# Feed-forward's quantisation of the gated activations: two ScalarE operations instead of two VectorE operations

## What is computed

```
def _act_quant(x):
    scale = 127.0 / jnp.clip(jnp.max(jnp.abs(x), axis=-1, keepdims=True), 1e-05)
    return jnp.clip(jnp.round(x * scale), -128.0, 127.0) / scale
def _bitlinear(x, w):
    return jnp.einsum('bsi,oi->bso', _act_quant(x), _weight_quant(w))
gate = jax.nn.silu(_bitlinear(x, w_gate))      # 256 -> 1024
up = _bitlinear(x, w_up)                       # 256 -> 1024
return _bitlinear(gate * up, w_down)           # 1024 -> 256
```

## Time and profile before

| | us |
|---|---|
| median of 3 runs | 7127.48 (7126.87 to 7132.86) |
| the profiled execution, its own time | 7131.26 |
| its span, first to last instruction | 7129.5 |
| TensorE busy | 5831.5 (82%) |
| VectorE busy | 5463.8 (77%) |
| ScalarE busy | 3784.8 (53%) |
| GpSimd busy | 2616.1 (37%) |
| mean granted clock of TensorE | 0.917 of full speed |

### The profile page before, as it was taken

How to read it: one execution, slowest core, us unless ns; L and a number is a source line. 1 busy time by engine, 2 the same in 40 slices (tenths; PEclk the granted TensorE clock), 3 DMA queues, 4 the chain that set the end, 5 groups by cost and what they waited for, 6 DMA issues and landing times. The chain is left out here.

```text
span 7129.5 us, 143478 instructions
## 1 busy us (share of the span) xinstructions
PE 5831.5 (82%) x54804; PEld 3904.2 (55%) x54914; DVE 5463.8 (77%) x12626; ACT 3784.8 (53%) x6869; POOL 2616.1 (37%) x2600
## 2 busy tenths in 40 slices
PE   6899898688888787876999999999118888888887
PEld 4666566454545455544666666666105666666655
DVE  6777777578888888887777777777657888888886
ACT  4666666444555555553565565556105555555554
POOL 0111111122222222232434434544315666656664
PEclk9999999888888888887999999999658999999998
DMA  1111111100000000000000000100100000000000
GB/s 54 37 44 40 42 38 37 43 15 23 23 20 23 20 23 19 24 21 26 29 25 27 30 27 24 32 27 22 35 17 24 18 27 21 22 27 18 27 27 12
DMA packets 140386, 194.36 MB, mean 27 GB/s; under 512 B 25808, under 2 KB 63696, under 8 KB 139344
## 3 DMA queue, kind: packets, MB, share of 16 engines
q1 hardware_dynamic: 139728, 185.26, 8.2%
HBM read 113.03 MB, written 72.18 MB: 26 GB/s over the span
## 5 line engine op out<-in xcount | busy, mean ns | idle before, releaser
L1079 DVE TENSOR_REDUCE Dmp<-pj 128x2 f32<-128x512 f32 x1024 | 647.1, 683 | 145.5 <-PE pj L794 143.4
L1079 DVE TENSOR_REDUCE Amp<-pj 128x2 f32<-128x512 f32 x1024 | 644.7, 683 | 136.0 <-PE pj L794 135.6
L1079 DVE TENSOR_REDUCE Cmp<-pj 128x2 f32<-128x512 f32 x1024 | 643.2, 683 | 90.0 <-PE pj L794 89.5
L932 ACT ACTIVATE Dpr<-st 128x512 f32<-128x512 f32 x1024 | 528.8, 603 | 314.4 <-PE st L729 313.5
L932 ACT ACTIVATE Apr<-st 128x512 f32<-128x512 f32 x1024 | 528.7, 602 | 288.2 <-PE st L729 286.5
L932 ACT ACTIVATE Cpr<-st 128x512 f32<-128x512 f32 x1024 | 529.5, 606 | 250.5 <-PE st L729 249.1
L1014 POOL TENSOR_SCALAR Bve<-Bmv 128x2 f32<-128x2 f32 x128 | 29.6, 231 | 1346.0 <-DVE Bmv L1145 1346.0
L1014 POOL TENSOR_SCALAR Ave<-Amv 128x2 f32<-128x2 f32 x64 | 14.7, 229 | 1141.2 <-DVE Amv L1145 1141.2
L990 POOL TENSOR_TENSOR Dnrm<-Dnrm,power 128x32 f32<-128x32 f32 x64 | 348.6, 5447 | 161.7 <-DVE Dnrm L1057 161.7
L729 PE MATMUL st<-Dq,Dk 32*128 32x256 f32 x4096 | 361.7, 433 | 51.0 <-DVE Dq L1086 40.4
L932 ACT ACTIVATE Bpr<-st 77x512 f32<-77x512 f32 x512 | 262.0, 593 | 191.5 <-PE st L729 190.8
(11 more groups left out here) (310 smaller groups left out, 15817.8 us busy)
## 6 DMA issues: line engine op xcount, KB each, us to landing
Ax0T<-in_xT SPq DMA_DIRECT2D x64, 256.0 KB, 2.6
Ax<-in_x SPq DMA_DIRECT2D x64, 256.0 KB, 2.9
x_A_scratch<-Ax SPq DMA_DIRECT2D x64, 256.0 KB, 2.0
Bx<-x_A_scratch SPq DMA_DIRECT2D x64, 256.0 KB, 2.9
x_B_scratch<-Bx SPq DMA_DIRECT2D x64, 256.0 KB, 2.0
Cx<-x_B_scratch SPq DMA_DIRECT2D x64, 256.0 KB, 2.8
x_C_scratch<-Cx SPq DMA_DIRECT2D x64, 256.0 KB, 2.0
Dx<-x_C_scratch SPq DMA_DIRECT2D x64, 256.0 KB
```

What stands on the lines that cost most here:

```text
L932: ck.tell(act.activation(dst, st[bank][0:n, :], ACT.Exp, scale=HD ** -0.5), "probs_ready", step)
L1079: ins = dve.tensor_reduce(dst, src, AX.X, ALU.max, negate=True)
```

## The change

In hq, VectorE stops after the scale (column 11) and the factor (column 10), which are now issued one behind the other without a link between, and signals scale_ready. ScalarE gets a part in hq: it waits for scale_ready, computes hid * scale + MAGIC in place with one ACTIVATE (Identity, scale and bias from SBUF), waits for it, and computes hid - MAGIC into hq with a second one. The upper bound of 127 is left away. MAGIC and -MAGIC lie in a new tile of two columns, filled in the setup. The place of hq in the list is what it was; on ScalarE all its later steps now stand behind it.

```
-        "hq": ["dve_step"] * 6 + ["hq_ready"],
+        "hq": ["dve_step"] * 3 + ["scale_ready", "hid_rounded", "hq_ready"],
...
+        rounding = sb("rounding", [P, 2])
...
+                pool.memset(rounding[:, 0:1], MAGIC)
+                pool.memset(rounding[:, 1:2], -MAGIC)
...
+                    elif kind == "hq":
+                        t = step[3]
+                        flat = hid[s][:].rearrange("p a b -> p (a b)")
+                        ck.wait("scale_ready", step)
+                        ck.tell(act.activation(flat, flat, ACT.Identity, scale=qsc[s][:, t, 11:12], bias=rounding[:, 0:1]),
+                                "hid_rounded", step)
+                        if t > 0:
+                            ck.wait("hqT_ready", ("hT", att, s, t - 1))
+                        ck.wait("hid_rounded", step)
+                        ck.tell(act.activation(hq[s][:], flat, ACT.Identity, bias=rounding[:, 1:2]), "hq_ready", step)
...
-                        link(ck, dve.tensor_scalar(q[:, 11:12], q[:, 9:10], q[:, 6:7], QMAX, ALU.mult, ALU.mult))
-                        link(ck, dve.tensor_scalar(q[:, 10:11], q[:, 8:9], wq_inv[:, 2:3], 1.0 / QMAX,
-                                                   ALU.mult, ALU.mult))
-                        link(ck, dve.tensor_scalar(flat, flat, q[:, 11:12], MAGIC, ALU.mult, ALU.add))
-                        if t > 0:
-                            ck.wait("hqT_ready", ("hT", att, s, t - 1))
-                        ck.tell(dve.tensor_scalar(hq[s][:], flat, MAGIC, QMAX, ALU.subtract, ALU.min), "hq_ready", step)
-                        ck.wait("hq_ready", step)
+                        dve.tensor_scalar(q[:, 11:12], q[:, 9:10], q[:, 6:7], QMAX, ALU.mult, ALU.mult)
+                        ck.tell(dve.tensor_scalar(q[:, 10:11], q[:, 8:9], wq_inv[:, 2:3], 1.0 / QMAX,
+                                                  ALU.mult, ALU.mult), "scale_ready", step)
+                        ck.wait("scale_ready", step)
```

## The result

The changed kernel takes 7558.2 us (7545.79 to 7566.17, 4 runs) against 7128.71 us of the kernel before: ratio 1.060, 95% interval 1.0582 to 1.0618, 430 us more. The forecast was 7423 us with a range of 7270 to 7560; the time lies at its upper end, where the prediction had put "the clock falls too" (7553). The profiled execution took 7566.17 us, its span is 7564.4.

The account below looks back on a forecast made before the run. Stage B was taken as bound by in-order waits between engines, not busy time, though VectorE leads at 86%. Eight place shifts sum to 18.5 us a turn, times 16 is 296 us: 7423 us against the median, range 7270 to 7560.

Parts of the forecast that it names:

- the clock falls too: Rival: longer TensorE idle stretches lower its stage B clock to 0.74, adding 130 us: 7553 us; chance 0.12.
- a: Stream 0, tile 0: ScalarE's exponentials and key copies, formerly done before the scale, now wait behind hq; shift 3.8 us.
- b: Stream 1, tile 0: hq, then a copy and the Tanh VectorE waits for, come later on ScalarE; shift 2.2 us.
- c: Stream 1, tile 1: hq delays two copies of transposed tiles that TensorE's down product waits for; 0.5 us.
- d: Stream 0, tile 1: hq fits into 4.28 us of ScalarE idle time; no shift, and VectorE's relief worth nothing.
- e: Stream 3, tile 0: hq delays the oT copy, Tanh and query copies that free TensorE's bank; shift 1.6 us.
- f: Stream 3, tile 1: hq delays the take copy and the Tanh behind it; shift 1.3 us.
- g: Stream 2, tile 0: four exponentials, on which products and takes hang, now come after hq and a copy; shift 4.9 us.
- h: Stream 2, tile 1: two oT copies that release TensorE's output products now stand behind hq; shift 4.2 us.
- the sum as read: Main case: the shifts of all eight places in stage B add up, giving 7340 to 7500 us; chance 0.60.
- Only the longer path: Rival: ScalarE's queue has more room, leaving only the longer path to each consumer, about 144 us: 7271 us; chance 0.17.
- Relief wins: Rival: ScalarE has slack at most places, so each hq gives back VectorE's 1.5 us: 6935 us; chance 0.06.

Follow-up runs that it names:

- bare wait: Kernel before with nothing moved; at hq ScalarE only waits until VectorE has made the scale, then goes on: 7289.97 us, ratio 1.0223.
- e10: The change at place a only, the other seven hq left on VectorE as in the kernel before: 7236.88 us, ratio 1.0158.
- e9: Kernel before without VectorE's two rounding operations, nobody making them, so the output is not the computation: 7119.3 us, ratio 0.9990.
- e7: The change at places d and h only, at h with ScalarE's part behind the two oT copies, otherwise the kernel before: 7129.62 us, ratio 0.9996.
- e12: The change at place a only, plus 14 extra TensorE products a turn just ahead of the stall there: 7188.82 us, ratio 1.0080.
- e3: Changed kernel plus 44 extra TensorE products a turn (14, 16 and 14) at three places where TensorE idles: 7458.01 us, ratio 1.0450.
- e4: Changed kernel with ScalarE doing its part of hq a few steps later in its list at five of eight places: 7226.52 us, ratio 1.0127.

## Why the prediction was right, and where it was short

**What is added and removed: right.** 1240 + 1147 = 2387 ns where 2.32 to 2.38 us were worked out; VectorE 188 us less; no table load.

**The eight places: the mechanism right, four sizes short.** Slip gained at each place in us a turn, by the starts of VectorE's instruction above. The last two columns are the bare wait and the changed kernel with TensorE kept busy, read in the same way.

| place | forecast | changed kernel | bare wait | TensorE kept busy |
|---|---|---|---|---|
| a | 3.8 | 4.7 | 2.5 | 4.2 |
| b | 2.2 | 2.2 | 0 | 2.2 |
| c, d | 0.5 | 4.0 | 2.2 | 2.9 |
| e | 1.6 | 1.8 | 0 | 0.8 |
| f | 1.3 | 1.3 | 0 | 1.4 |
| g | 4.9 | 6.6 | 3.6 | 4.8 |
| h | 4.2 | 6.7 | 2.0 | 4.2 |
| turn | 18.5 | 27.3 | 10.3 | 20.5 |

b, e and f came as read, and with the stalls filled g and h do too. The queue's part can also be read in the changed kernel where the clock doesn't enter: g starts its exponentials 4.8 us later (102.05 - 83.20 from the anchor, less the 14.0 before it; 4.9 forecast). At h the output products start with a slip of 120.07 - 94.73 = 25.3, some 4.7 more than after g (4.2 forecast), and end with 27.3: the last 2.0 are their own slowness.

**The step that failed** is the last one before the total: "What this reading can miss: TensorE's clock". The sum took every product at its old speed, kept the clock's price out and gave it 0.12, with 0.60 for the sum as read. The prediction's own terms make TensorE wait some 4 us longer at a, g and h in each turn, and at 0.87 the stage was already paying. Filling three stalls takes 6.8 of the 27.3 us away (100 us of the run). That much at least is the clock's, since the extra products can only have cost time themselves. The second step that failed is c: 0.5 us was read there and 4.0 measured. Of these 2.0 appear also in e10, which leaves c alone and has slow products there; the rest is ScalarE's list and the wait for hq itself, not divided further.

**The case that came true had its price partly by luck.** "The clock falls too" supposed a clock of 0.74, 260 us more of TensorE and half of them on the path: +130. Measured were 0.81 and 161 us, and at least 100 us back when the stalls were filled: a smaller fall, more of it on the path. And the 130 us also stood in for what the sum lacked at c.

**The range** held the time by 2 us, and only because it was drawn to take in this rival; the band for the sum as read, 7340 to 7500, did not. "Only the longer path" (7271) fell: the waits at a, g and h had no more room than read. "Relief wins" (6935) fell doubly: e9 shows that even a free relief is worth 7 us. That the prediction counted VectorE's 1.5 us as next to nothing was right; even the 0.9 us at h that the expectation of e7 gave it did not show.

**The profile after:** rows of 1.22 and 1.13 us expected, 1.24 and 1.15 found; stage 2155 expected, 2290 found; VectorE's share 65% expected, 62% found; L1186's idle time of several hundred us released by the Tanh: 305.7 in the stage.

## What to carry to other kernels

Before work is moved to an engine with spare time, read for each place what stands behind it on that engine and when that used to run: here the wait in front of the moved work cost 157 us by itself, and the same work a few steps later in the list lost 94 us instead of 430. A share of 86% doesn't make an engine the bound; leave its work out for once and see what it is worth. Where a change makes TensorE wait for some us in each turn, put the slower products behind the stall into the sum, and look for more of them further on.

## What the runs showed of the hardware

TensorE ran the products behind stalls of 4.28 to 5.01 us at 1.2 GHz (pairs at 1.03 to 1.06 us for 0.59, sixteen output products 5.70 for 3.72), and in the run with the bare wait behind one of 2.83 us too (a pair 1.03). The length of the stall alone does not tell: behind 2.04 us the output products ran at full speed (3.72), and in the kernel before a pair behind 2.02 us is slow:

```profile
1998.63 0.59 PE L708 MATMUL pj<-ident_b,Bxq 128*128 128x128 bf16 x4 [2.02 <-DVE Bmp L1079]
1999.01 1.06 PE L847 MATMUL pj<-wg,BxqT 128*128 128x512 bf16 x2
```

Not expected: the slow stretch that comes back 19 to 22 us after the stall at a (down products 2.54 for 1.92), and that useless products, put where TensorE will stall, can shorten a kernel by 100 us. What brings the second stretch about is left open. With the change at a alone it goes when the stall is filled (e12); with the change at all eight places and the same fill it does not (e3, where the down products take 3.07 us), and in e4 it stands there without a stall of that length at a.
